# Int8 rows transposed two to a 16-bit word, and five queues reordered for it

## The reference, cut to what matters

```python
y = einsum('bij,bkj->bik', x, weight[ids])          # x (8,256,1024), weight[id] (1024,1024), f32
h = layernorm(y, gamma, beta)
h = fake_quant(h) @ fake_quant(w1).T + b1
h = gelu(h)                                          # exact form
h = fake_quant(h) @ fake_quant(w3).T + b3
out = x + h
# fake_quant(v): s = max(max|v| over the row / 127, 1e-8); clip(round(v / s), -127, 127) * s
```

## Time and profile before

| | |
|---|---|
| three runs | 373.23, 369.0, 368.7 us, median 369.0 |
| profiled execution | span 372.5 us from the first to the last instruction; the run of 373.23 us is the one nearest to it |
| PE busy | 341.4 us of the span (92%), 1854 matmuls and transposes |
| POOL busy | 263.4 us (71%) |
| DVE busy | 285.5 us (77%) |
| ACT busy | 227.1 us (61%) |
| HBM | 58.74 MB read, 8.39 MB written, 180 GB/s over the span |

### The profile page before, as it was taken

One profiled execution on the slowest core, in us unless ns is written; L12 is line 12 of the kernel. 1 busy time (PEld: TensorE's weight loads), 2 busy tenths in 40 slices (PEclk: granted clock), 3 DMA queues, 4 the chain that ended last, 5 costly groups with the idle time before them and its releaser, 6 DMA issues.

```text
span 372.5 us, 5769 instructions
## 1 busy us (share of the span) xinstructions
PE 341.4 (92%) x1854; PEld 235.9 (63%) x1880; DVE 285.5 (77%) x344; ACT 227.1 (61%) x232; POOL 263.4 (71%) x164
## 2 busy tenths in 40 slices
PE   6898899996976999999999999999899989999885
PEld 6787788754763666666665666566566666674442
DVE  1459698886946777798778886888779687999866
ACT  2433476854888647773777658755777477625651
POOL 1402259841998579995999599968997699946831
PEclk9999999999899999999999999999999999999989
DMA  6999998695950899539971999099925990150014
GB/s 186 352 347 352 410 280 164 147 246 117 241 99 0 199 276 218 100 119 294 221 154 63 299 223 203 0 268 244 220 56 158 288 229 0 58 171 1 0 55 172
DMA packets 46203, 67.35 MB, mean 181 GB/s; under 512 B 2918, under 2 KB 37734, under 8 KB 46186
## 3 DMA queue, kind: packets, MB, share of 16 engines
q1 hardware_dynamic: 46186, 67.14, 68.8%
HBM read 58.74 MB, written 8.39 MB: 180 GB/s over the span
## 4 chain that ended last, share of the span: by engine, by line
POOL 41%; issue 22%; DMA 13%; DVE 11%; PE 7%; SPq 3%; ACT 2%; POOLq 0%; DVEq 0%
POOL y L458 8%; POOL x_res L474 7%; POOL o L466 6%; POOL y L460 5%; DMA x_res<-in_L_ffn_w 5%; POOL a L478 4%; POOL x_lo L483 4%; POOL o L469 3%; DMA w_scale_row<-in_L_ffn_w 3%; PE t_ps L1134 2%; DMA h_r<-in_L_cond_weight 2%; DVE x_nat L917 2%; DMA x_t<-in_L_ffn_b 2%; DVE wq_max L861 2%; DMA w_nat<-in_L_cond_weight 2%
## 5 line engine op out<-in xcount | busy, mean ns | idle before, releaser
L1080 PE MATMUL a_ps<-w_hi,x_hi 128*128 128x512 f32 x256 | 107.5, 420 | 2.4 <-DVE w_lo L794 1.2
L1082 PE MATMUL a_ps<-w_hi,x_lo 128*128 128x512 f32 x256 | 100.8, 394 | 0.0
L1081 PE MATMUL a_ps<-w_lo,x_hi 128*128 128x512 f32 x256 | 100.7, 393 | 0.0
L1134 PE MATMUL f_ps<-w_q,q_t 128*128 128x512 bf16 x377 | 88.1, 379 | 9.7 <-ACT q_t L627 8.2
L1134 PEld LDWEIGHTS f_ps<-w_q,q_t 128*128 128x128 bf16 x400 | 37.1, 98 | 57.5 <-ACT q_t L627 12.5
L803 DVE STREAM_TRANSPOSE t_ps<-w_nat 128x1024 f32<-128x1024 f32 x48 | 57.5, 1238 | 11.7 <-DMA w_nat<-in_L_cond_weight 11.5
L809 DVE TENSOR_TENSOR w_lo<-t_ps,w_hi 128x1024 fp32r<-128x1024 f32 x48 | 57.2, 1219 | 8.9 <-ACT w_hi L574 8.7
L574 ACT ACTIVATE w_hi<-t_ps 128x1024 fp32r<-128x1024 f32 x48 | 49.0, 1023 | 21.9 <-DVE t_ps L803 21.1
L1080 PEld LDWEIGHTS a_ps<-w_hi,x_hi 128*128 128x128 f32 x256 | 48.5, 189 | 15.7 <-ACT y L589 3.2
L1082 PEld LDWEIGHTS a_ps<-w_hi,x_lo 128*128 128x128 f32 x256 | 48.5, 189 | 10.7
L1081 PEld LDWEIGHTS a_ps<-w_lo,x_hi 128*128 128x128 f32 x256 | 48.6, 190 | 9.0
(11 more groups left out here) (151 smaller groups left out, 503.1 us busy)
## 6 DMA issues: line engine op xcount, KB each, us to landing
w_nat<-in_L_cond_weight SPq DMA_DIRECT2D x96, 256.0 KB, 6.5
x_res<-in_x SPq DMA_DIRECT2D x7, 1024.0 KB, 6.3
out<-o SPq DMA_DIRECT2D x14, 512.0 KB, 3.1
x_nat<-in_x SPq DMA_DIRECT2D x24, 256.0 KB, 9.9
w_nat<-in_L_cond_weight SPq DMA_DIRECT2D x10, 512.0 KB, 8.9
w_q<-in_L_ffn_w SPq DMA_DIRECT2D x4, 512.0 KB, 7.9
h_r<-in_L_cond_weight SPq DMA_DIRECT2D x4, 512.0 KB, 6.7
w_scale_row<-in_L_ffn_w SPq DMA_DIRECT2D x3, 512.0 KB, 10.3
```

The source lines that it names most:

```text
L1080: pe.matmul(ps, hi, w_hi[:, u, c], start=begin, stop=False)
L1081: pe.matmul(ps, hi, w_lo[:, u, c], start=False, stop=False)
L1082: last = pe.matmul(ps, lo, w_hi[:, u, c], start=False, stop=end)
L1134: last = pe.matmul(ps[:, half, :], q[:, c, :], w[:, c, half_of(half)], start=c == 0, stop=c == CB - 1)
```

## The change

**Bytes.** The three rounding steps multiply by the inverse scale and write int8, 1024 bytes for a row of 1024, in place of f32 with the large constant; the constant's addition and its `bias=` operand are gone (ScalarE's is then the default, GpSimd's second operation is none). Rows of h lie in the first kilobyte of a row of `h_r`, rows of g in the second (the last g tiles in the third), prep tiles at the head of their own slot.

**Words.** `transpose_tile` reads two neighbouring bytes as one 16-bit word and makes four 128x128 transposes in place of eight. Two tiles of h fill one PSUM bank instead of two. The taking copies read int8 from PSUM with a step of two bytes and write the same bf16 tiles as before, contiguous; the same number of elements.

**Order.** The TensorE order of the loop and of the last period stays. In the loop, ScalarE, VectorE and GpSimd are reordered as below. In the start, the loads, the TensorE, ScalarE, VectorE and GpSimd queues are reordered; of SP's the diff shows most, of the others a part. On GpSimd `round_prep` of tile 7 goes ahead of `normalisers_of(0)`, tile 8 ahead of `scale_and_shift(0, 0)`, `add_b1(0, 0)` ahead of `low_x(2, 0)`. On ScalarE `take_prep` is spread otherwise between the splits, and `take_scale_row(0)` comes ahead of `copy_y(1, 0)`. On VectorE `max_prep` and `scales_prep` of the first two parts come earlier.

```diff
+        bytes_of = [h_r[:, t, :].bitcast(I8) for t in range(TT)]
+        h_8 = [row[:, 0:D] for row in bytes_of]
+        g_8 = [row[:, D:2 * D] for row in bytes_of]
+        g_8_last = [row[:, 2 * D:3 * D] for row in bytes_of]
+        prep_8 = [slot.bitcast(I8)[:, 0:D] for slot in prep_slot]
...
-        def transposed(bank, dtype):
-
-            return bank.bitcast(dtype).rearrange("p (c k) -> p c k", k=P)
+        WORDS = D // PACK // PACK
+
+        def words_of(bank, t=0):
+
+            return bank[:, WORDS * t:WORDS * (t + 1)].bitcast(BF16).rearrange("p (c k) -> p c k", k=P)
+
+        def bytes_in(bank, tiles=1):
+
+            return bank[:, 0:WORDS * tiles].bitcast(I8).rearrange("p (c k b) -> p c b k", k=P, b=PACK)
+
+        def blocks_in(q):
+
+            return q.rearrange("p (c b) k -> p c b k", b=PACK)
 
...
             load_first_x((0,))
             sp.wait_ge(ids_loaded, 16)
+            load_first_x((1,))
             load_first_unit(0)
-            load_first_x((1,))
             load_first_unit(1)
             load_rows()
             load_first_unit(2)
-            load_prep((2, 4))
+            load_first_unit(3, (1,))
+            load_prep((2,))
+            load_prep((4,))
+            load_prep((0,))
+            load_prep((1,))
+            load_prep((3,))
+            load_first_unit(3, (0,))
+            load_second_x()
             load_rows_of_w((0,))
-            load_prep((0,))
-            load_first_unit(3, (1,))
-            load_prep((1,))
-            load_first_unit(3, (0,))
-            load_prep((3, 5))
+            load_prep((5,))
+            load_prep((6,))
             load_rows_of_w((1,))
-            load_prep((6,))
-            load_rows_of_w((2, 5))
-            load_second_x()
+            load_rows_of_w((2,))
+            load_rows_of_w((5,))
             load_prep((11,))
             load_rows_of_w((3,))
-            load_prep((7, 8, 9))
-            load_rows_of_w((4, 6, 7))
-            load_prep((12, 10))
+            load_prep((7,))
...
+            load_prep((10,))
+            load_x(2)
             load_unit(2, 1)
-            load_x(2)
             load_unit(2, 0)
-            load_prep((15, 14))
             load_unit(2, 2)
+            load_prep((15,))
+            load_prep((14,))
             load_prep((13,))
+            load_residual(0)
             load_unit(2, 3)
-            load_residual(0)
+            load_unit(3, 0)
+            load_unit(3, 1)
...
-                    pool.tensor_scalar(prep_slot[i], prep_slot[i], wq_inv[:, i:i + 1], magic[:],
-                                       ALU.mult, ALU.add).then_inc(wq_rounded, 1)
+                    pool.tensor_scalar(prep_8[i], prep_slot[i], wq_inv[:, i:i + 1], None, ALU.mult).then_inc(wq_rounded, 1)
 
             def period(p):
                 low_x(p + 1, 0)
                 add_b1(p - 1, 0)
                 residual(p - 1)
+                low_x(p + 1, 1)
                 normalisers_of(p)
-                low_x(p + 1, 1)
                 add_b1(p - 1, 1)
-                for t in range(TT):
-                    scale_and_shift(p, t)
-                for t in range(TT):
-                    finish(p - 1, t)
+                scale_and_shift(p, 0)
+                scale_and_shift(p, 1)
+                finish(p - 1, 0)
...
-                act.activation(h_r[:, t, :], rows_of(f)[:, t, :], ACT.Identity, scale=h_inv[:, t:t + 1], bias=magic[:]
-                               ).then_inc(h_rounded, 1)
+                act.activation(h_8[t], rows_of(f)[:, t, :], ACT.Identity, scale=h_inv[:, t:t + 1]).then_inc(h_rounded, 1)
...
-                act.activation(q_t[:].rearrange("p t c k -> p (t c k)"),
-                               f_ps[:].bitcast(I16).rearrange("p h n -> p (h n)"), ACT.Copy).then_inc(h_t_ready, 1)
+                act.activation(blocks_in(q_t[:].rearrange("p t c k -> p (t c) k")), bytes_in(f_ps[:, 0], TT), ACT.Copy
+                               ).then_inc(h_t_ready, 1)
...
-                act.activation(a[:, t, :], a[:, t, :], ACT.Identity, scale=g_inv[:, t:t + 1], bias=magic[:]
-                               ).then_inc(g_rounded, 1)
+                act.activation(g_8[t], a[:, t, :], ACT.Identity, scale=g_inv[:, t:t + 1]).then_inc(g_rounded, 1)
 
             def take_g(f, t):
                 act.wait_ge(g_transposed, TT * f + t + 1)
-                act.activation(q_t[:, t], transposed(f_ps[:, 0], I16), ACT.Copy).then_inc(g_t_ready, 1)
+                act.activation(blocks_in(q_t[:, t]), bytes_in(f_ps[:, 0]), ACT.Copy).then_inc(g_t_ready, 1)
...
-                    act.activation(w_q[i // RT][:, :, rows_of_tile], transposed(f_ps[:, i % 2], I16), ACT.Copy
+                    act.activation(blocks_in(w_q[i // RT][:, :, rows_of_tile]), bytes_in(f_ps[:, i % 2]), ACT.Copy
                                    ).then_inc(wq_ready, 1)
...
-                both(p + 1, 0)
+                split_w(p + 1, 0, 0)
                 take_h(p - 1)
                 split_x(p + 1, 0)
-                both(p + 1, 1)
+                split_w(p + 1, 0, 1)
+                split_w(p + 1, 1, 0)
                 gelu(p - 1, 0)
                 copy_y(p, 1)
+                split_x(p + 1, 1)
+                split_w(p + 1, 1, 1)
                 round_g(p - 1, 0)
-                split_x(p + 1, 1)
+                take_g(p - 1, 0)
                 normalise(p, 0)
+                split_w(p + 1, 2, 0)
+                split_w(p + 1, 2, 1)
+                gelu(p - 1, 1)
                 normalise(p, 1)
-                split_w(p + 1, 2, 0)
-                take_g(p - 1, 0)
-                gelu(p - 1, 1)
-                split_w(p + 1, 2, 1)
+                scale_ffn2(p - 1, 0)
                 round_g(p - 1, 1)
-                scale_ffn2(p - 1, 0)
+                split_w(p + 1, 3, 0)
+                split_w(p + 1, 3, 1)
+                take_g(p - 1, 1)
                 round_h(p, 0)
-                split_w(p + 1, 3, 0)
-                take_g(p - 1, 1)
-                split_w(p + 1, 3, 1)
                 round_h(p, 1)
                 copy_y(p + 1, 0)
                 scale_ffn2(p - 1, 1)
...
-                both(transpose_w, p + 1, 0)
-                both(low_w, p + 1, 0)
+                transpose_w(p + 1, 0, 0)
+                transpose_w(p + 1, 0, 1)
                 transpose_x(p + 1)
-                both(transpose_w, p + 1, 1)
+                low_w(p + 1, 0, 0)
                 rescale1(p - 1, 0)
-                both(low_w, p + 1, 1)
+                low_w(p + 1, 0, 1)
+                transpose_w(p + 1, 1, 0)
+                transpose_w(p + 1, 1, 1)
+                low_w(p + 1, 1, 0)
                 scales_g(p - 1, 0, a[:, 0, :], 0)
                 statistics(p, 1)
                 mean_and_variance(p)
                 rescale1(p - 1, 1)
-                both(transpose_w, p + 1, 2)
+                low_w(p + 1, 1, 1)
+                transpose_w(p + 1, 2, 0)
+                transpose_w(p + 1, 2, 1)
                 low_w(p + 1, 2, 0)
+                low_w(p + 1, 2, 1)
                 scales_g(p - 1, 1, a[:, 1, :], 1)
-                low_w(p + 1, 2, 1)
+                transpose_w(p + 1, 3, 0)
+                transpose_w(p + 1, 3, 1)
                 scales_h(p, 0, 0)
-                both(transpose_w, p + 1, 3)
                 scales_h(p, 1, 1)
-                both(low_w, p + 1, 3)
+                low_w(p + 1, 3, 0)
+                low_w(p + 1, 3, 1)
                 statistics(p + 1, 0)
...
-            both(transpose_w, 2, 0)
+            transpose_w(2, 0, 0)
+            scales_prep(2)
+            transpose_w(2, 0, 1)
+            statistics(1, 0)
             low_w(2, 0, 0)
+            low_w(2, 0, 1)
+            rescale1(0, 0)
             transpose_w(2, 1, 0)
-            statistics(1, 0)
-            low_w(2, 0, 1)
+            transpose_w(2, 1, 1)
             low_w(2, 1, 0)
-            rescale1(0, 0)
-            transpose_w(2, 1, 1)
             transpose_w(2, 2, 0)
+            rescale1(0, 1)
             max_prep((13, 14))
-            rescale1(0, 1)
             max_prep((15,))
             scales_prep(3)
+            statistics(1, 1)
+            scales_g(0, 0, a[:, 0, :], 0)
+            mean_and_variance(1)
             low_w(2, 1, 1)
-            scales_g(0, 0, a[:, 0, :], 0)
-            statistics(1, 1)
-            mean_and_variance(1)
             transpose_w(2, 2, 1)
             low_w(2, 2, 0)
...
-            def transpose_tile(src, bank, done):
-                halves = src.bitcast(BF16).rearrange("p (k two) -> p k two", two=2)[:, :, 0]
-                blocks = transposed(bank, BF16)
-                for c in range(CB):
-                    last = pe.transpose(blocks[:, c, :], halves[:, c * P:(c + 1) * P], ident_16[:])
+            def transpose_tile(src, blocks, done):
+                words = src.bitcast(BF16)
+                for c in range(CB // PACK):
```

(95 more changed lines are left out.)

82 lines of the change are left out of this document (44 added, 38 removed).

## The result

The changed kernel takes 367.2 us (median of 20 runs) beside 370.3 for the kernel before: a ratio of 0.9887, interval 0.9858 to 0.9916, 4.2 us less. This ratio, like all that follow, leaves out the executions that fell in the slower of the program's two states, which is why it says more than the two medians over all runs, 3.1 us apart. The forecast was 353, its range 345 to 365.

A forecast was written before the change was run, and what follows sets the result against it. The prediction took TensorE's instruction queue, plus a few waits from ScalarE's order, to bound the loop. Its terms, -8.3 - 7 - 1 = -16.3 us from a median of 369.0, gave a forecast of 353 us, range 345 to 365.

The forecast's parts named there:

- Costs that the trace does not show: Assumed prices: byte rounding 1.12 us on ScalarE, 1.2 on GpSimd (bounds 1.2 and 2.4), taking copies 0.83 ns an element.
- Term 3: Start: fewer transposes, the wait for rescale1(0, 1) and low-clock time gone, less new waits: -7 us, bounds -11 and -2.
- Term 2: Loop's order: waits for take_g go, 0.3 us for copy_y stays; period 38.0 us, five periods -8.3 with fewer transposes.
- Term 1: Loop: each of a period's 4 tiles goes from 8 to 4 transposes, 0.85 us a period, all on PE's path.
- Rival A: Order gives nothing; waits regrow where transposes were, take_g's 0.2 us margin missed: 363 us, chance 0.12.
- Term 4: Last period: fewer transposes and shorter rounding where DVE, ACT and PE take turns: -1 us, bounds 0 and -3.
- Rival B: Taking copies: a byte-stepped read costs three times as much, making the kernel slower at 388 us; chance 0.10.
- Rival C: Start's loads: PE starves for batch 1's weight or the clock falls again, start +3, total 363 us; chance 0.10.

The follow-up runs named there:

- e1: Separate kernel of single 128x1024 instructions on idle engines: GpSimd's lone multiply takes 2.84 us into f32 as into bytes, multiply then add 1.19 us.
- e6: Changed kernel with GpSimd's rounding as multiply, then add of a zero, still into bytes: 355.8 us, ratio 0.9624.
- e3: Kernel before, every queue in its old order, with the bytes alone: 380.8 us, ratio 1.0279.
- e10: Kernel before in its old order, with the bytes and GpSimd's rounding as multiply, then add of a zero: 367.3 us, ratio 0.9913.
- e4: Changed kernel's order with the old formulas (f32 with the large constant, eight transposes): 359.3 us, ratio 0.9707.
- e8: Changed kernel with both the added zero in GpSimd's rounding and the early residual load: 352.5 us, ratio 0.9500.
- e7: Changed kernel with the residual's load issued earlier, GpSimd's residual step writing into y_first so x_res is free: 363.6 us, ratio 0.9806.
- e9: Changed kernel's order with the old formulas (f32, eight transposes) and the early residual load: 357.6 us, ratio 0.9661.
- e2: Changed kernel with the 16 prep tiles alone back to f32 and eight transposes, h and g staying bytes: 358.0 us, ratio 0.9663.

## Why the prediction was wrong, point by point

**Costs that the trace does not show, the rounding on GpSimd: the step that failed.** "1202 ns with two operations; bounds 1.2 and, as for its two-input step, 2.4 us. I take 1.2." The row was of another instruction: the change removes the addition, and a lone multiply takes 2.84 us on this engine whatever it writes (e1). It lay outside my bounds, because I took the row with the addition for the price without it, and a two-input step for the worst. Its cost in the changed kernel is 9.7 us (e6), in the old order 13.5 (e3 to e10), the clock that falls with it counted in. I had worked out that at 2.4 the start would gain about 1; it gained 0.3 in the traces, and ended at 125.8 us where I had called anything past 119 a sign of being wrong. The mechanism was right there, and had no share in the chances, since no rival stood for it.

**Term 3, the start, -7.** Inside its bounds once the rounding costs what I assumed: 116.4 in e6 against 126.1, -9.7 in the traces. But it did not come from the parts that I had added up, so that it is near is partly luck. The order alone made -6.6 (e4), where my sum had 3.1 + 1.8 - 2.3 = 2.6 for it; the transposes, which I had at 4.3, are left with 3.1. The wait for `rescale1(0, 1)` went, as forecast. The 1.8 us for the clock did not come: the stretch at 1.2 GHz only moved. In the changed kernel it stands behind the wait of 2.8 us for `scale_ffn2`, which ends at 115.7; in e6 it stands at 100 to 106. Windows of the changed kernel (length, busy us of PE, PEld, DVE, ACT, POOL, clock, DMA):

```profile
118.00:120.00 2.00, 2.00 (x6) 0.72 (x5) 2.00 (x3) 1.92 (x4) 1.92 (x2) 0.50 0.00 0
120.00:122.00 2.00, 2.00 (x9) 0.85 (x8) 2.00 (x4) 0.28 (x1) 1.24 (x1) 0.81 0.00 0
```

What else the order removed from the start was not taken apart.

**Term 2, the loop's order, -8.3 with term 1.** The changed kernel's loop gave -6.9, e8's -11.7, at my bound for no wait left. The walk was right in what it removed: with the order alone the period is 38.1 to 38.7 with eight transposes, no wait for `take_g`. Its last sentence is true and stops short: "The SP queue in the loop is untouched; its first load waits for GpSimd's last `finish`, which hangs on ffn2 of tile 1 as before." The load's start stayed, 7.0 us behind the start of `piece(p, 2, 0)` in both kernels, and the need for it moved 2.4 us ahead, since `add_b1` of tile 0 starts at 10.6 and no longer at 13.0. So GpSimd waits 0.4 to 2.2 us for it in four of the five periods and the copies follow. It costs 0.8% in the changed kernel and 1.2% beside the fast form (e7, e8).

**Term 1, -0.85 us a period.** Sized right (0.75 in e9 to e8, both bound by PE), but in the changed kernel it went into the wait for `copy_y`: five periods of 191.8 us with the bytes and 191.6 without. Rival A had named this outcome, waits that regrow where the transposes were, but laid it to `take_g`'s margin; that margin held (0.3 us of waits in the loop), and the cause was a transfer.

**Term 4, -1.** 47.6 against 47.7 in these traces, both with a stretch at the lower clock: nothing gained. Of the 1.7 us that PE saves there 1.1 went into longer waits, 3.2 us against 2.7 for the g tile and 1.0 against 0.4 for an h tile; where the other 0.6 went was not traced. The rest is 46.0 in others; see below for the 1.6 us between them.

**Rival B** is out: a byte step costs ScalarE nothing (1023 ns). The sentence of the Trainium skill, "SBUF — State Buffer" (the DMA port swizzle), that a non-contiguous access in PSUM slows matmuls is not contradicted, since these copies are no matmuls. The rule of the Trainium skill, "ScalarE: Activation LUTs" (what the load of a table costs), one element a cycle whatever the function, for f32 and bf16, agrees with the int8 copies too: 1877 - 1023 = 854 ns for 1024 elements more, 0.83 ns each. **Rival C** did not show where I had put it: PE's waits for weights before 50 us add up to under 1 us. That the clock would fall again in the start did come, later and behind other waits.

The sum itself, -16.3, is not far from what the kernel gives with the rounding mended (e6, -13.9 by its ratio) and with the load mended too (e8, -18.5). By the terms above that is partly luck, since the start came from other parts and the last period gave nothing at an equal clock. Two smaller slips: I started from 369.0, the median of three runs, and over 20 it is 370.3; and 0.68 and a third of A's 0.12 and C's 0.10 make 0.75, not 0.77.

## What to carry to other kernels

Price an instruction that a change makes simpler as if it were new: take a row of the very form, and where there is none, measure it by itself before believing that fewer operations cost less. When a reordering brings a step forward, follow each of its operands back to its transfer and ask what starts that transfer; a load that is issued by an event which did not move becomes the next wait. A saving on the engine that bounds a loop is only as large as the distance to the next chain: write down that chain's length before adding the saving up. And compare the average granted clocks of two kernels before laying all of their difference to one step.

## What the runs showed of the hardware that I had not expected

GpSimd's `tensor_scalar` on 128x1024 f32: multiply-add and multiply-multiply 1.19 to 1.20 us into f32, bf16, int16 or int8 (1.04 to 1.11 with constants in the instruction), a lone multiply or add 2.79 to 2.85, multiply-minimum and add-subtract 3.78 to 3.79. VectorE does the same multiply into bytes in 0.75 us. Why the pairs differ is not shown.

The last period has a wait of 3.2 us for a g tile in every trace with bytes, of 2.7 in those without. In the changed kernel the granted clock fell to its lower level (1.2 GHz) in the stretch behind it, as in the kernel before and in e2, e3, e4, e7 and e9; in e8, with the same wait, it stayed at the upper one, as in e6 and e10:

```profile
351.20:353.20 2.00, 2.00 (x10) 0.98 (x8) 0.95 (x2) 1.49 (x2) 1.62 (x1) 0.58 0.00 0
```

```profile
336.80:338.80 2.00, 1.95 (x13) 1.01 (x12) 1.90 (x7) 0.91 (x2) 0.00 (x0) 1.00 0.00 0
```

That fits the 1.6 us between rests of 47.6 and 46.0. What decides it was not tried.

The starts have such stretches too, at places that differ from trace to trace: none in e2, one in the kernel before, the changed kernel, e4, e6, e9 and e10, two in e3, e7 and e8. Where there is one, the windows of 2 us that it touches add up to 1.7 us of full speed lost (0.84, 0.50 and 0.81 in the changed kernel). The average granted clock, over the executions behind the ratios, is 0.984, 0.978 and 0.981 in the three kernels with the lone multiply (changed, e3, e7), and 0.990, 0.991 and 0.993 in those that differ from them by the added zero alone (e6, e10, e8). So that instruction costs TensorE twice: the waits for it, and slower work behind the waits. How many microseconds fall to the second is an estimate; no run changed the clock alone.
